# A delta-rule attention phase: new orders and PSUM banks around the first level of the block inverse

## The reference, cut to what matters

```python
q = causal_conv(x @ Wq); k = causal_conv(x @ Wk); v = causal_conv(x @ Wv)   # 4 taps
q = silu(q); k = silu(k) * D ** -0.5; v = silu(v)                            # 16 heads of 128
alpha = sigmoid(x @ Wa + ba); beta = sigmoid(x @ Wb + bb)
def step(St, (q_, k_, v_, a_, b_)):                                          # per head, 512 steps
    err = St @ k_ - v_
    Sn = a_ * St - b_ * outer(err, k_)
    return Sn, Sn @ q_
o = (o - mean(o)) * rsqrt(var(o) + 1e-5) * ln_w + ln_b                       # per head
o = (o * sigmoid(x @ Wg)) @ Wo
```

## Time and profile before

| | |
|---|---|
| median of 3 runs | 3017.93 us (3017.1 to 3018.24) |
| the profiled execution | 3018.13 us, its span 3016.3 us |
| TensorE busy | 2824.9 us (94%) |
| VectorE busy | 1837.2 us (61%) |
| ScalarE busy | 1206.1 us (40%) |
| GpSimd busy | 611.9 us (20%) |
| the 16 delta rounds | from 1124.5 us to about 2675 us |

### The profile page before, as it was taken

The page is one execution under the profiler, slowest core; times in us unless marked ns, Lnnn a source line. Parts: engine busy times, 40 slices in busy tenths (PEclk is TensorE's granted clock), DMA queues, the critical chain, the costliest instruction groups (busy, mean ns, idle before and its releaser), DMA issues. The chain is left out here.

```text
span 3016.3 us, 37740 instructions
## 1 busy us (share of the span) xinstructions
PE 2824.9 (94%) x13038; PEld 1584.4 (53%) x13039; DVE 1837.2 (61%) x4645; ACT 1206.1 (40%) x2214; POOL 611.9 (20%) x669
## 2 busy tenths in 40 slices
PE   6999989989999968999999999999999999999787
PEld 3444434445665444666556665566655665554232
DVE  5767752011111557877787778877778777547586
ACT  4545521012212354444554445544454445422232
POOL 1111201301110403033321333123330233200000
PEclk9999989999999978999999999999999999999899
DMA  3100151031211821002101021000111001226213
GB/s 126 47 15 28 42 199 78 22 125 63 69 63 56 322 104 68 29 20 80 53 33 43 15 71 64 36 29 30 71 57 43 29 29 67 86 93 233 70 46 98
DMA packets 78423, 215.22 MB, mean 71 GB/s; under 512 B 12065, under 2 KB 12977, under 8 KB 69681
## 3 DMA queue, kind: packets, MB, share of 16 engines
q1 hardware_dynamic: 57472, 165.79, 15.2%
q0 software_dynamic: 9264, 28.36, 2.9%
q10 hardware_dynamic: 11520, 18.92, 1.7%
HBM read 156.25 MB, written 56.79 MB: 71 GB/s over the span
## 5 line engine op out<-in xcount | busy, mean ns | idle before, releaser
L2281 DVE SCALAR_TENSOR_TENSOR c_conv<-c_ps_pj,c_conv_t,c_conv 128x511 f32<-128x511 f32 (+2 forms) x495 | 368.0, 746 | 85.6 <-ACT c_conv L2119 74.0
L1812 POOL TENSOR_SCALAR c_gate<-c_gate 128x512 f32<-128x512 f32 x64 | 40.8, 638 | 934.3 <-ACT c_gate L2111 934.3
L1903 PE MATMUL c_ps_pj<-c_w_g,c_xs 128*128 128x512 f32 x512 | 227.7, 592 | 0.0
L1886 PE MATMUL c_ps_pj<-c_xs,c_w_v 128*128 128x512 f32 x480 | 225.8, 593 | 0.0
L1886 PE MATMUL c_ps_pj<-c_xs,c_w_k 128*128 128x512 f32 x480 | 217.9, 597 | 6.1 <-DMA c_xs<-xt_d 6.1
L1886 PE MATMUL c_ps_pj<-c_xs,c_w_q 128*128 128x512 f32 x360 | 195.1, 677 | 0.3
L2119 ACT ACTIVATE c_conv<-c_ps_pj,c_conv_t 128x512 f32<-128x512 f32 x165 | 127.8, 774 | 87.8 <-PE c_ps_pj L1886 85.8
L2300 DVE TENSOR_TENSOR c_block_X<-c_block_X,c_block_t 128x126 f32<-128x126 f32 (+22 forms) x496 | 143.5, 289 | 17.0
L2296 DVE TENSOR_TENSOR c_block_t<-c_block_L,c_block_X 128x126 f32<-128x126 f32 (+22 forms) x496 | 138.6, 279 | 17.0
L1903 PEld LDWEIGHTS c_ps_pj<-c_w_g,c_xs 128*128 128x128 f32 x512 | 93.6, 190 | 100.0 <-issue 100.0
L2171 ACT ACTIVATE c_err<-c_negL 32x128 f32<-32x128 f32 x256 | 78.6, 307 | 153.1 <-DVE c_negL L2365 148.3
(11 more groups left out here) (518 smaller groups left out, 5817.8 us busy)
## 6 DMA issues: line engine op xcount, KB each, us to landing
c_G<-cum_d SPq DMA_DIRECT2D x16, 1024.0 KB, 4.7
c_xs<-xt_d SPq DMA_DIRECT2D x16, 1024.0 KB, 4.8
ot_d<-c_oT ACTq DMA_DIRECT2D x64, 256.0 KB, 2.0
b_w_gu<-in_w_gu SPq DMA_DIRECT2D x8, 1408.0 KB, 20.8
y_slots<-x_y SPq DMA_DIRECT2D x40, 256.0 KB, 2.0
a_x<-in_x SPq DMA_DIRECT2D x8, 1024.0 KB, 6.3
d_x<-x SPq DMA_DIRECT2D x32, 256.0 KB, 2.9
d_switch<-in_switch_w SPq DMA_DIRECT2D x4, 2048.0 KB, 17.1
```

Source lines behind the costliest of these rows:

```text
L1886: mm = e.matmul(bank_of[xb][u][:, :], w["kqv"[u // HG]][:, k, (u % HG) * DH:(u % HG + 1) * DH], xs[xb][:, k, :], start=(k == 0), stop=(k = ...
L1903: mm = e.matmul(pj[(xb + i) % 2][:, :], xs[xb][:, k, i * P:(i + 1) * P], w["g"][:, k, :], start=(k == 0), stop=(k == KD - 1))
L2281: e.scalar_tensor_tensor(oc, bank_of[buf][u][:, 0:SEQ - s], conv_t[buf][:, m, h, TAPS - 1 - s:TAPS - s], oc, ALU.mult, ALU.add).then_inc(c ...
```

## The change

- `diagonal_inverse`: the first two steps and the last, where one factor has a single column or row, become one instruction each. A function `meanwhile` runs between its transpose and its steps: the taps of unit 2.
- VectorE's front: unit 11's taps move from the end of a round behind kd of the next round's first chunk; the taps of units 0 and 1 stand at chunks 1 and 2. The copy out of the r bank goes ahead of the taps of unit 5.
- The root of the variance moves to ScalarE (`norm_root`: Ln and Exp, with the table set `natural_log_exp_and_others`), behind the second chunk's corner cut; 15 small instructions of VectorE go, and `norm_offset` stays at the last chunk.
- TensorE's front: unit 1 is halved over chunks 1 and 2, and unit 2 goes behind the last chunk's kk, ahead of gate 0. So the fourth kk comes one unit sooner.
- Banks: gate 1 goes into the z bank, unit 3 into the r bank, with the waits that belong to it; unit 6 now waits for gate 2's tanh only.
- ScalarE: the taps of units 0, 1 and 2 at chunks 0, 2 and 3; the tap of unit 5 behind the Z copies instead of ahead of T's spreading.
- GpSimd: the wait for `T_turned` stands ahead of the gates' scaling, in every round.
- The level of 128: the products of the second `z_half` and the first `r_half` alternate, and the second half of unit 7 is cut into two quarters around them.

```diff
-    SUB_STEPS = 1 + 1 + 2 * (BB - 1)
+    SUB_STEPS = 1 + 1 + 2 * (BB - 1) - 3
-    RSTD_STEPS = 16
+    RSTD_STEPS = 3
+        gate_bank = lambda xb, i: z_ps if i == 1 else pj[(xb + i) % 2]
+            bank_of[s][HG - 1] = r_ps
...
             def a_round(r, buf, last=False):
+                e.wait_ge(T_turned, r + 1)
                 finish_gates(r, buf)
                 if after_first(r):
-                    e.wait_ge(T_turned, r + 1)
...
-                        if u in (HG - 1, HG) and gates_before:
-                            e.wait_ge(g_copied, TPB * (q - 1) + u)
+                        if u == HG - 1:
+                            e.wait_ge(kd_done, (TPB - 1) * q)
+                        elif u == HG:
+                            e.wait_ge(g_copied, TPB * q)
                         elif u == HG + 1:
-                            if gates_before:
-                                e.wait_ge(A_done, TPB * q)
-                        elif u in (HG + 2, HG + 3):
+                            e.wait_ge(A_done, TPB * q)
+                        elif u == HG + 2:
+                            e.wait_ge(g_copied, TPB * q - 1)
+                        elif u == HG + 3:
                             e.wait_ge(conv_step, TAP_STEPS * (CONVS * q + u))
...
                     if c == TPB - 1:
+                        next_unit(2)
...
-                        next_unit(c)
+                        if c == 0:
+                            next_unit(0)
+                        else:
+                            next_unit(1, (c - 1,))
...
                     e.wait_ge(T_done, 2 * (r + 1))
+                    e.wait_ge(g_copied, TPB * r + 2)
...
                     e.wait_ge(zl_done, 4 * r + 2)
+                    if not last:
+                        e.wait_ge(conv_step, TAP_STEPS * (CONVS * (r + 1) + HG + 2))
...
-                for p in range(PAIRS):
-                    z_half(p)
-                for p in range(PAIRS):
-                    r_half(p)
-                next_unit(HG + 3, (1,))
+                for i in range(2 * HG):
+                    z_half(0, i)
+                next_quarter(HG + 3, 2)
+                for i in range(2 * HG):
+                    z_half(1, i)
+                    r_half(0, i)
+                next_quarter(HG + 3, 3)
+                for i in range(2 * HG):
+                    r_half(1, i)
...
+            def norm_root(q):
+
+                step = q * RSTD_STEPS
+                e.wait_ge(o_mean, NM * q + NM)
+                e.activation(o_ve[:, :], o_mv[:, :, 1], ACT.Ln, bias=con["eps"][:, :]).then_inc(o_rstd, 1)
+                e.wait_ge(o_rstd, step + 1)
+                e.activation(o_rs[:, :], o_ve[:, :], ACT.Exp, scale=-0.5).then_inc(o_rstd, 1)
...
-                e.preload_act_table_set("exp_and_others")
+                e.preload_act_table_set("natural_log_exp_and_others")
...
-                    if c < TPB - 1:
-                        next_tap(c)
+                    if c != 1:
+                        next_tap(max(c - 1, 0))
+                    if c == 1 and after_first(r):
+                        norm_root(r - 1)
...
                 next_tap(HG)
-                next_tap(HG + 1)
...
                     e.activation(Z[down, :, :, up], z_block[b][down], ACT.Copy).then_inc(zl_done, 1)
+                next_tap(HG + 1)
...
-            def diagonal_inverse(r):
+            def diagonal_inverse(r, meanwhile):
...
+                meanwhile()
+                made = step + 2
                 for i in range(BB - 1):
                     n, k = BB - 1 - i, i // 2 + 1
+                    left, top, below = block_L[:, i + 1:BB, i], block_X[:, i, 0:k], block_X[:, i + 1:BB, 0:k]
+                    e.wait_ge(sub_step, made)
+                    if k == 1:
+                        e.scalar_tensor_tensor(below[:, :, 0], left, top, below[:, :, 0], ALU.mult, ALU.add).then_inc(sub_step, 1)
+                        made += 1
+                        continue
+                    if n == 1:
+                        e.scalar_tensor_tensor(below[:, 0, :], top, left, below[:, 0, :], ALU.mult, ALU.add).then_inc(sub_step, 1)
+                        made += 1
+                        continue
...
+                    if 0 < c < TPB - 1:
+                        next_taps(c - 1)
                     if after_first(r):
+                        if c == 0:
+                            taps(r, buf, CONVS - 1, None)
                         norm_part(r - 1, c)
-                    if c < TPB - 1:
-                        next_taps(c)
...
-                diagonal_inverse(r)
-                for u in range(HG - 1, HG + 2):
+                diagonal_inverse(r, lambda: next_taps(2))
+                for u in range(HG - 1, HG + 1):
                     next_taps(u)
...
+                next_taps(HG + 1)
                 next_taps(HG + 2)
...
                 norm_stats(r, TPB - 1)
-                next_taps(CONVS - 1)
...
             def tail(r, buf):
                 a_round(r, buf, None, last=True)
+                e.preload_act_table_set("natural_log_exp_and_others")
+                norm_root(r)
```

## The result

| | before | changed |
|---|---|---|
| median | 3017.51 us (4 runs) | 2964.68 us (4 runs, 2960.74 to 2965.37) |
| profiled execution, its span | 3018.13, 3016.3 us | 2965.37, 2963.5 us |
| ratio to before, 95% interval | | 0.9824 (0.9807 to 0.9841) |

The change takes 52.8 us off; the forecast was 61.7 off, 2956 us, with 2942 to 2980 for 8 times in 10. The time is inside. One step of the reasoning that led there was nevertheless wrong: what TensorE had waited for.

What follows compares the result with a forecast made beforehand. TensorE's own work bounds the kernel, beside about 2 us waiting for T and 1.6 us of clock fall a round. Rounds 2 to 15 48.9, first 11.0, last 0.65, tail 1.1: 61.7 off 3018.1 gives 2956 us; range 2942 to 2980.

Steps and rivals of the forecast that it cites:

- Part 2: VectorE's chain of the inverse: shortened from 19.4 to 17.3 us, so TensorE's 2.03 us wait for T goes.
- The layout by hand: Front of a round: new order laid out with old durations; TensorE loses 0.97 us, through with unit 5 at 1857.15.
- the three waits: TensorE's new front: 0.35 us for A, 0.57 for unit 11's taps, 0.63 at the third chunk's kk.
- The rival with 0.10: Rounds 2 to 15: the clock still falls once a round, costing 14 x 1.62 us; 2979 us, chance 0.10.
- those with a late T: T 1.4 to 4 us later: 2980 to 3015 us, chance 0.06; later by much: 3034 us, chance 0.04.
- 1.6 + 0.65: First round, beside its 8.7 us wait: 1.6 us from the clock's fall and 0.65 from the second level saved.
- The second level: The 64x64 passes: second z and first r pass overlap wholly, 0.95 us off, net 0.65 us a round.
- the rival in which they don't: Second level: the two passes don't overlap, 16 x 0.95 = 15 us lost; 2971 us, chance 0.11.
- 0.1 left open: Second level: a 0.86 us quarter unit leaves 0.1 us uncovered before ScalarE's Z copy, back about 0.95 us after a pass.
- Price nothing: Banks: gate 1 in the z bank and unit 3 in the r bank cost no time; the cover is 2.5 us.
- 0.65 + 1.1: Last round gains 0.65 us; the tail loses its 1.1 us wait for the last round's output.

Runs made afterwards that it cites:

- the scaling experiment: Kernel before with one edit: GpSimd waits for T_turned ahead of the gates' scaling in every round; 3008.93 us, ratio 0.9973.
- the four parts together: Kernel before with scaling behind the chain, fused steps, root on ScalarE and alternating second level; old front and old tap place; 3006.36 us, ratio 0.9962.
- the late fourth kk: Changed kernel with TensorE's old order of units 0, 1 and 2, so the fourth chunk's kk comes one unit later; 2965.92 us, ratio 0.9828.

## Why the prediction came out right, and where it was wrong

**The wait for T and its clock: right in size, wrong in cause.** Part 2 said that the chain on VectorE set T and that shortening it (fused steps, no held instructions) would take the wait away; the move of unit 5's tap stood there in a bracket. The runs showed that in the kernel before ScalarE's queue was last: T's spreading stood behind a tap that waits for TensorE's own unit 5. The chain was about 0.4 us ahead of it. T's time in the changed kernel was worked out rightly because the tap is moved in it; but that reasoning gave the move no share of the gain, and that the one edit on which the others hang was in the bundle is luck as far as it goes. The move is necessary (0.9824 becomes 1.0015 without it). It is not enough alone (1.0004), and with the scaling behind the chain it reaches 0.9844. Whether another saving of the chain's time would do in the scaling's place was not tried, nor was the changed kernel with the scaling put back. The chain itself lasts 17.5 us, forecast 17.3: the scaling took 1.4 us off as worked out, the fused steps 0.5 and not 0.7.

**The front.** The layout by hand held: the products start 46.32 us into the round, forecast 1857.15 - 1810.87 = 46.28; T has 1.38 us to spare, forecast 1.35; the three waits are there, 0.8 us in the rows of one round (1.55 in issue time was the forecast; a row's idle time starts at the end of the drain).

**The clock.** Right: 1.00 in every round from the second to the fifteenth, and in their fronts too, in spite of the waits there. The rival with 0.10 is refuted, and so are those with a late T, which has 1.38 us to spare.

**The first round** gained 11.5 us (112.16 to 100.65), forecast 11.0, and its chain fell to 17.5 us, as worked out. The terms offset each other in part: the products start 9.0 us sooner (8.7 forecast), and the way from them to the product with R fell from 17.08 to 14.47 us, 2.6 for the forecast 1.6 + 0.65, since the fall of the clock had cost 2.3 us there.

**The second level: mis-sized.** The passes do overlap wholly: a pass of z and a pass of r together take 1840.00 to 1841.08, so the rival in which they don't is refuted. But from the first z pass to the product with R it now takes 1843.21 - 1837.88 = 5.33 us where it took 5.65, so 0.32 us are gained and not 0.65. The term that failed is the price of changing between small and large products, for which I had put down 0.2 us and 0.1 left open. The row of before in which the half unit follows the four passes:

```profile
1872.96 1.98 PE L1886 MATMUL c_ps_pj<-c_xs,c_w_q 128*128 128x512 f32 x4
```

By the starts the four passes took 1872.96 - 1869.13 = 3.83 us and the half unit 1.82. Now the three passes take 1.07 + 1.08 + 1.07 = 3.22 us, 0.61 less and not 0.95, and the two quarters 1.05 + 1.06 = 2.11 us, 0.29 more. So the changes cost about 0.6 us and not 0.3. Another 0.1 us is lost just behind: the way from the product with R to the next round is 31.78 us after and 31.68 before, and it is 31.8 in every run with the alternating second level and 31.7 in every one without it.

**The banks: right in the sum, and not free to leave out.** "Price nothing" fits the changed kernel: its list of waits has none at gate 1, at unit 3 or at the second 32x32 pass. But with unit 2's taps behind the transpose, gate 1 in its old bank costs 1.33 us a round. Its new bank is a need of the new front. Unit 3's bank was not tried by itself.

**The new front: no gain of its own found here.** With it the products start 46.32 us into the round, and 45.41 with the old one and the old banks; the waits in the rows are 0.8 us a round against 0.5. The version without it is 0.8 us a round faster. T's larger margin, which it was to keep, isn't needed once the tap, the scaling, the fused steps and the root are in place: the 0.4 us left are enough in the rounds 2 to 15, and only the first round has a wait for T (0.7 us).

**The rest of the miss.** Forecast 61.7 us off, measured 52.8. From the profiled executions: 14 x 3.06 = 42.9 us in the rounds 2 to 15 against 48.9, and nearly all of this is the second level: 14 x 0.33 = 4.6 in it and 14 x 0.1 = 1.4 behind it, which I had left unchanged. The first kk came 1.8 us later than in the execution before, ahead of everything that was changed; in the changed kernel's second profile it came at 1124.87, so this is the execution's. In the last round and the tail together 0.3 us were gained and not 0.65 + 1.1: when VectorE's output came earlier, ScalarE's copy out of the bank was the next to be late (0.83 us).

## What to carry to other kernels

A list of waits names the instruction that released the waiter, not what held that instruction up: before an edit is aimed at the long chain behind it, look at what stood in front of it in its own engine's queue, and at what that waits for. When two feeders are late by nearly the same time, undo an edit in the full version as well as trying it alone in the old one; alone, both looked worthless here (0.9973 with only the first round's gain, and 1.0004), together they are 1.6%, and it was the undoing of the tap's move that showed what hung on it. And once a bundle is faster, take its parts out: this one contained a new front that cost 10 us (2963.74 against 2953.93).

## What the runs showed of the hardware

The clock's fall behind a wait is not a property of the wait alone. The same wait of 2.03 us, with TensorE busy 1.37 of 3.40 us, was followed by a granted clock of 1.00 in the second round of the scaling experiment and by 0.52 in its ninth:

```profile
1275.20:1278.60 3.40, 1.37 (x60) 0.94 (x60) 3.29 (x6) 2.86 (x5) 3.32 (x6) 1.00 0.00 0
1278.60:1282.00 3.40, 3.40 (x87) 2.08 (x80) 3.29 (x6) 3.28 (x6) 3.32 (x3) 1.00 0.02 5
...
1945.60:1949.00 3.40, 1.37 (x48) 0.80 (x48) 3.29 (x6) 2.72 (x5) 3.32 (x6) 0.98 0.00 0
1949.00:1952.40 3.40, 3.40 (x31) 1.74 (x26) 3.29 (x5) 3.03 (x6) 3.32 (x3) 0.52 0.02 5
```

Of fourteen rounds with this wait the clock fell in fourteen in the kernel before, in thirteen in the scaling experiment, in twelve in the four parts together and in eleven with the tap put back. A wait of 1.7 us (the move alone) was followed by a fall in fourteen of fourteen, one of 0.3 to 0.45 us (the move with the scaling, and the late fourth kk) in none.

In the kernels in which it falls in nearly every round, most rounds settle at nearly the same length, 95.54 to 95.60 us (before, the scaling, the fused steps, the root, and the move alone), each with one fall behind the wait. The move alone is among them though its products start 0.35 us sooner. The one round of the scaling experiment without a fall took 93.99 us. Why this length, and whether a small saving can be hidden by it, was not tried; the rounds of the four parts together did not settle there (95.3 to 95.5 us).

GpSimd's work beside VectorE's chain showed its price plainly in the first round: with 11.3 us of it beside the chain the chain lasted 25.6 us, and 18.0 us in the scaling experiment, whose only edit puts that work behind it (17.5 in the changed kernel, with the fused steps). The Trainium skill (SBUF — State Buffer, SBUF: two separate sides) says that of a VectorE operation with two SBUF inputs and a GpSimd operation that reads SBUF the one that starts first holds the shared ports for its whole length and the other is blocked. The trace agrees as far as it goes: the 0.49 us of the earlier trace rows end with GpSimd's instruction, and the chain's stretch of 7.6 us is less than the 11.3 us beside it.
